# Picking 32 more early columns of the first edge stage with one-hot matmuls in the set-up

## The reference

```python
xl = (x @ W_l + b_l).reshape(n, HEADS, C)
xr = (x @ W_r + b_r).reshape(n, HEADS, C)
e = (edge_attr @ W_e).reshape(-1, HEADS, C)
g = jax.nn.leaky_relu(xl[src] + xr[dst] + e, NEG_SLOPE)
logits = jnp.einsum('ehc,hc->eh', g, att)
ex = jnp.exp(logits - segment_max(logits, dst)[dst])
alpha = ex / (segment_sum(ex, dst)[dst] + 1e-16)
out = segment_sum(xl[src] * alpha[..., None], dst)
```

## Time and profile before

| | |
|---|---|
| median of 3 runs | 5896.49 us (5888.83 to 5905.95) |
| profiled execution | 5837.42 us, span 5835.3 us |
| set-up | 0 to 135.8 us |
| edge stage 0 | from 135.8 us, last chunk near 1394 us |
| GpSimd in stage 0 | 752 gathers, 731.9 us busy, 482.6 us idle |
| TensorE over the whole program | 67% busy, VectorE 69%, ScalarE 36%, GpSimd 62% |

### The profile page before, as it was taken

One profiled execution on the slowest core, in us unless ns is written; L12 is line 12 of the kernel. 1 busy time (PEld: TensorE's weight loads), 2 busy tenths in 40 slices (PEclk: granted clock), 3 DMA queues, 4 the chain that ended last, 5 costly groups with the idle time before them and its releaser, 6 DMA issues. The chain is left out here.

```text
span 5835.3 us, 55453 instructions
## 1 busy us (share of the span) xinstructions
PE 3918.1 (67%) x16273; PEld 2718.5 (47%) x16273; DVE 4024.6 (69%) x5761; ACT 2088.4 (36%) x3734; POOL 3621.4 (62%) x3384
## 2 busy tenths in 40 slices
PE   2555555564599999999999557767733536655561
PEld 1333333333488888888888423333312422222221
DVE  3566666675599999999998557778763346555553
ACT  0455555553144444444444124444431211111111
POOL 6655555663577777777776366666655255655554
PEclk6788888886799999999999568888865767777775
DMA  7566666663588888888886333333332631211111
GB/s 276 199 220 214 217 215 223 224 224 119 203 318 311 312 316 311 315 316 309 319 309 260 83 107 108 111 110 114 101 91 88 254 101 52 57 52 53 53 51 47
DMA packets 359630, 1074.10 MB, mean 184 GB/s; under 512 B 100998, under 2 KB 124354, under 8 KB 315012
## 3 DMA queue, kind: packets, MB, share of 16 engines
q1 hardware_dynamic: 241524, 852.49, 39.0%
q0 software_dynamic: 102208, 156.10, 10.4%
q10 hardware_dynamic: 15696, 63.31, 3.2%
HBM read 678.05 MB, written 392.57 MB: 183 GB/s over the span
## 5 line engine op out<-in xcount | busy, mean ns | idle before, releaser
L1874 PE MATMUL COLS<-CF,XF 128*128 128x256 f32 x6272 | 1485.4, 380 | 6.3 <-DVE XF L1982 6.3
L1874 PEld LDWEIGHTS COLS<-CF,XF 128*128 128x128 f32 x6272 | 1134.7, 190 | 130.3 <-DVE XF L1982 6.7
L1137 ACT ACTIVATE OUT<-SC 128x576 f32<-128x576 f32 (+3 forms) x392 | 576.5, 1471 | 1333.4 <-DVE SC L1072 678.9
L1020 POOL DMA_INDIRECT G<-xl_tab,SRC x752 | 731.9, 973 | 482.6 <-DVE TURNS L1054 272.2
L1841 POOL DMA_INDIRECT G<-x_tab,SRC x784 | 780.9, 996 | 234.6 <-issue 216.0
L1020 POOL DMA_INDIRECT G<-rel_tab,REL x672 | 639.1, 951 | 424.6 <-DVE SC L1072 227.2
L1020 POOL DMA_INDIRECT G<-kv_tab,SRC x608 | 599.7, 986 | 372.8 <-issue 187.6
L1451 PE MATMUL PICK<-HOT,X 125*128 125x512 bf16 x2200 | 571.0, 418 | 276.0 <-issue 147.7
L1623 PE MATMUL MADE<-XM,W 128*128 128x512 f32 x896 | 529.5, 747 | 328.4 <-DVE XM L1711 261.8
L1261 PE MATMUL WK<-B2R,ONER 128*128 128x512 f32 x392 | 258.6, 660 | 524.1 <-ACT WKV L1314 483.5
L1451 PEld LDWEIGHTS PICK<-HOT,X 125*128 125x128 bf16 x2200 | 228.0, 105 | 603.6 <-issue 396.6
(11 more groups left out here) (310 smaller groups left out, 7086.0 us busy)
## 6 DMA issues: line engine op xcount, KB each, us to landing
SHB<-ea9t SPq DMA_DIRECT2D x196, 1024.0 KB
wkv_tab<-WKV SPq DMA_DIRECT2D x98, 1024.0 KB
WKV<-wkv_tab SPq DMA_DIRECT2D x98, 1024.0 KB
scan<-OUT SPq DMA_DIRECT2D x196, 288.0 KB
scan<-OUT ACTq DMA_DIRECT2D x98, 576.0 KB
rel_tab<-YS SPq DMA_DIRECT2D x50, 1024.0 KB
RAW<-spread SPq DMA_DIRECT2D x196, 256.0 KB
spread_q<-ZQ SPq DMA_DIRECT2D x98, 512.0 KB
```

The costliest lines, as they stand in the source:

```text
L1020: pool.indirect_dma_start(out=self.G[0][d][:, c, :], out_offset=None, in_=tab, in_offset=bass.IndirectOffsetOnAxis(ap=index[:, at:at + 1], ...
L1137: nc.scalar.activation(self.OUT[d][:, :, 0:WD], SC[b][:, 0:WD, 1:1 + C].rearrange("p r j -> p j r"), ACT.Copy).then_inc(self.copied_out, 1)
L1874: nc.tensor.matmul(acc, XF[b][:, k, edges_], CF[:, k, :], start=(k == 0), stop=False)
```

## The change

EARLY_T becomes every chunk from 1 to 95 that is no multiple of three: 64 chunks in place of 32. The stage then has 720 gathers and 64 place_early copies. XEARLY doubles. Its first 32 columns are gathered in the set-up as before. The other 32 (t = 49 to 95) are picked in the set-up, in four batches of 8 columns (1024 edges):

- SP broadcasts the 1024 source indices of a batch to all partitions (SRC8, 512 KB), ScalarE narrows them to 16 bits (ID16), and VectorE compares them with each of the 25 groups of nodes into HOT, five groups at a time, two buffers.
- x is split in three bfloat16 pieces, which lie in X3 as [high, middle] and [low, blank]. TensorE multiplies each of the two pairs by the one-hot columns, two halves of 512 columns: 20 matmuls in a pick, 5 picks in a batch, 400 matmuls in all. They are summed in PICK, which takes the two PSUM banks that FB and PR had.
- ScalarE copies PICK to TURNED (take), TensorE multiplies it by the weights stacked twice (project_picked), and VectorE adds b_l (make_picked).

The orders of the engines change with it. TensorE does picks 0 and 1 between the second and the third group of table rows, pick 2 before the last group, and all others behind the rows, with the turning and projecting of the gathered columns among them.

```diff
-EARLY_T = [2 + 3 * i for i in range(EARLY)]
+EARLY_PICKED = 4
+EARLY_T = [t for t in range(1, NCH - 2) if t % 3]
...
+                    def load_sources(i):
+                        if i:
+                            sp.wait_ge(narrowed, i)
+                        sp.dma_start(SRC8[:, :], src_first[i:i + 1, :].to_broadcast([P, 8 * P])).then_inc(src8_in, 16)
...
                         sp.wait_ge(seg_in[part], 16 * (k1 - k0))
+                        if part == 1:
+                            load_sources(1)
                         blank_spread(sp, range(3 + 2 * part, 5 + 2 * part))
                     blank_spread(sp, range(3 + 2 * len(PARTS), BLANKS))
+                    for i in range(2, EARLY_PICKED):
+                        load_sources(i)
                     sp.wait_ge(rows_made, 7)
...
+                    def compare(at):
+                        i, q = divmod(at, 5)
+                        v.wait_ge(narrowed, i + 1)
+                        if at == 0:
+                            v.wait_ge(node_known, 1)
+                        if at >= 2:
+                            v.wait_ge(read, at - 1)
+                        for k in range(5 * q, 5 * q + 5):
+                            ins = nc.vector.tensor_scalar(HOT[at % 2][N, k % 5, :], ID16[i % 2][N, :], NODE_F[N, k:k + 1],
+                                                          None, ALU.is_equal)
+                        ins.then_inc(compared, 1)
...
+                        if part == 0:
+                            v.wait_ge(x_high, 1)
+                            nc.vector.tensor_tensor(REST[:, :, :], X[:, :, :], X3[:, :, 0, 0:64], ALU.subtract)\
+                              .then_inc(x_rest, 1)
+                            compare(0)
+                        if part == 1:
+                            v.wait_ge(x_middle, 1)
+                            nc.vector.tensor_tensor(X3[:, :, 1, 0:64], REST[:, :, :], X3[:, :, 0, 64:128], ALU.subtract)\
+                              .then_inc(x_low, 1)
+                            compare(1)
...
+                        if u == 4:
+                            compare(2)
...
+                    for at in range(3, 5 * EARLY_PICKED):
+                        compare(at)
+                        if at % 5 == 1:
+                            make_picked(at // 5 - 1)
+                        if 12 <= at <= 15:
+                            make_early(at - 12)
+                    make_picked(EARLY_PICKED - 1)
...
+                    narrow(0)
+                    act.wait_ge(x_rest, 1)
+                    nc.scalar.activation(X3[:, :, 0, 64:128], REST[:, :, :], ACT.Copy).then_inc(x_middle, 1)
+                    narrow(1)
+                    act.wait_ge(x_low, 1)
+                    take(0)
+                    narrow(2)
+                    take(1)
+                    narrow(3)
...
+                    def pick(at):
+                        i, q = divmod(at, 5)
+                        pe.wait_ge(compared, at + 1)
+                        if q == 0 and i >= 1:
+                            pe.wait_ge(taken, i)
+                        for k in range(5 * q, 5 * q + 5):
+                            for piece in range(2):
+                                for half in range(2):
+                                    edges_ = slice(512 * half, 512 * half + 512)
+                                    last = nc.tensor.matmul(PICK[:, edges_], X3[N, k, piece, :], HOT[at % 2][N, k % 5, edges_],
+                                                            start=(k == 0 and piece == 0), stop=(k == K - 1 and piece == 1))
+                        last.then_inc(read, 1)
...
+                    project_rows(0)
+                    project_rows(1)
+                    pe.wait_ge(t_copied, 2)
+                    pe.wait_ge(blank, 1)
+                    pe.wait_ge(x_low, 1)
+                    pick(0)
+                    pick(1)
+                    for u in range(2, len(GROUPS)):
+                        if u == len(GROUPS) - 1:
+                            pick(2)
+                        project_rows(u)
+                    for at in range(3, 5 * EARLY_PICKED):
+                        pick(at)
+                        if at % 5 == 0:
+                            project_picked(at // 5 - 1)
+                        if 12 <= at <= 15:
+                            project_early(at - 12)
+                        if 11 <= at <= 14:
+                            turn_early(at - 11)
+                    project_picked(EARLY_PICKED - 1)
```

More of the change, by code:

```diff
@@ L58 @@
 EARLY = 32
-EARLY_T = [2 + 3 * i for i in range(EARLY)]
+EARLY_PICKED = 4
+EARLY_T = [t for t in range(1, NCH - 2) if t % 3]
 EARLY_FIRST = 4
 ROWS0_AT = [sum(C - (q in EARLY_T) for q in range(t % 4, t + 1, 4)) for t in range(NCH)]
-assert EARLY_T[-1] < NCH - 2 and EARLY % 8 == 0
+assert EARLY_T[-1] < NCH - 2 and EARLY % 8 == 0 and len(EARLY_T) == EARLY + 8 * EARLY_PICKED
 BATCHES3 = 14
@@ L243, in graph_kernel @@
         early_rows = ExitStack()
-        XEARLY = sb("XEARLY", [P, EARLY, 64], F32, early_rows)
+        XEARLY = sb("XEARLY", [P, len(EARLY_T), 64], F32, early_rows)
         BLANKS = J // 56
@@ L440, in _, with make_early @@
                     st.then(nc.vector.tensor_scalar(CARRY_AT[:, :], ST[:, 4, 2:3], float(NPAD), None, ALU.add))
[L442 to L450, removed]
-                    for i in range(EARLY // 8):
+                    def make_early(i):
                         v.wait_ge(early_done, i + 1)
@@ L465, in _, with narrow, take, copy_early @@
                           .then_inc(x_copied, 1)
-                    for i in range(EARLY // 8):
+                    nc.scalar.activation(X3[:, :, 0, 0:64], X[:, :, :], ACT.Copy).then_inc(x_high, 1)
+                    def narrow(i):
+                        act.wait_ge(src8_in, 16 * (i + 1))
+                        if i >= 2:
+                            act.wait_ge(compared, 5 * (i - 1))
+                        nc.scalar.activation(ID16[i % 2][:, :], SRC8[:, :], ACT.Copy).then_inc(narrowed, 1)
+                    def take(i):
+                        act.wait_ge(read, 5 * i + 5)
+                        if i >= 1:
+                            act.wait_ge(pick_done, i)
+                        nc.scalar.activation(TURNED, PICK[:, :], ACT.Copy).then_inc(taken, 1)
+                    def copy_early(i):
                         act.wait_ge(early_turned, i + 1)
@@ L495, in _, with project_picked, turn_early @@
                         last.then_inc(rows_done, 1)
-                    pe.wait_ge(w_early_in, 16)
-                    pe.wait_ge(x_early_in, 16 * EARLY)
-                    for i in range(EARLY // 8):
-                        if i >= 1:
+                    def pick(at):
[10 more added lines that the diff above has]
+                        last.then_inc(read, 1)
+                    def project_picked(i):
+                        pe.wait_ge(taken, i + 1)
+                        if i == 0:
+                            pe.wait_ge(weights_stacked, 1)
+                        else:
+                            pe.wait_ge(pick_made, i)
+                        for c in range(8):
+                            last = nc.tensor.matmul(PT[0][:, 64 * c:64 * c + 64], TURNED[:, c * P:(c + 1) * P], WL2[:, :],
+                                                    start=True, stop=True)
+                        last.then_inc(pick_done, 1)
+                    def turn_early(i):
+                        if i == 0:
+                            pe.wait_ge(w_early_in, 16)
+                            pe.wait_ge(x_early_in, 16 * EARLY)
+                        else:
                             pe.wait_ge(early_copied, i)
@@ L2592 @@
         "basis": a["L3_gnn_basis"],
-        "src_early": np.stack([src_cols[:, t * C + C - 1] for t in EARLY_T], axis=1),
+        "src_early": np.stack([src_cols[:, t * C + C - 1] for t in EARLY_T[:EARLY]], axis=1),
+        "src_first": np.stack([src_cols[:, t * C + C - 1] for t in EARLY_T[EARLY:]]).reshape(EARLY_PICKED, 8 * P),
         "w_early": w_early,
```

49 lines of the change are left out of this document (45 added, 4 removed).

## The result

The changed kernel has a median of 5972.62 us (5961.46 to 5979.04, 4 runs) against 5895.81 for the kernel before on the same chip: the ratio is 1.0127, 95% interval 1.0106 to 1.0148, or 77 us more. The forecast of slower was right, and 5972 lies in the range, but the step was put at 26 us, a third of what came. The profiled execution has a span of 5959.6 us.

The account below looks back on a forecast made before the run. GpSimd ends the set-up; no engine bounds stage 0 throughout, but GpSimd's gathers count one for one in its cycle. Set-up +66 and stage 0 -40 give +26 on the 5896.49 median: 5922 us, range 5865 to 5980.

Parts of the forecast that it names:

- What goes: Edge stage 0: 32 gathers fewer on GpSimd, 40 us saved, with bounds of 0 and 110.
- If the two pauses stay, each cycle shortens by 1.25 us: Stage 0's three-chunk cycle: with GpSimd's pauses of 7.33 and 1.58 us unchanged, 32 x 1.25 = 40 us go.
- Rival B: Stage 0: gathers aren't in the cycle, so fewer only lengthen GpSimd's pause; net +43 to +66 us, chance 0.15.
- What comes: Set-up: picking adds 43 us at full pace, plus 17 and 6 for TensorE's second pace, +66 in all.
- Table rows at 82: Set-up: the last table rows, ending at 77.15 before, end at about 82 with pick(2) ahead of them.
- Late signals beside the first run of gathers: Set-up, GpSimd's run until 91.2: TensorE's slow pace loses between nothing and 12 us; 6 taken.
- unknown price: Set-up: matmuls beside GpSimd's back-to-back runs might go 2.1 to 3.5 us apart, as in stage 2; 17 + 6 us.
- The objection that the table rows of before ran without gaps: Set-up: rows 2 to 6 ran beside gathers without slow-pace gaps, which spoke against that pace there; no size of its own.
- Late signals beside the scatters: Set-up, scatters ending at 134: 18 us in which 7 or 8 matmuls pass where 85 would; 17 us lost.
- D: Set-up: matmuls mostly run at the lower clock because of waits between groups; net about +75 to +90 us, chance 0.10.
- A (full pace in the set-up): Set-up: TensorE keeps its full pace, set-up +43, net +3 us, so 5900 and no difference; chance 0.20.
- C (rarer stalls): Stage 0: stalls come once per four chunks, 110 us less there, net -44, so 5852; chance 0.15.

Follow-up runs that it names:

- setup_rest: The changed kernel with a GpSimd memset of 128x1100 behind every fifth XEARLY gather and every fifth set-up scatter; 1.0074 of the kernel before, set-up 197.3 us.
- stage_all_seven: The kernel before with 7 gathers in each of chunks 1 to 95 of stage 0, placed rows being copies; 0.9859 of the kernel before, stage 0 1211.3 us.
- reorder: The changed kernel with compares from 13 ahead of make_early, pick and compare 2 behind the table rows, table stores before the last index load; 1.0092 of the kernel before.
- no_scatter: The changed kernel without the 25 set-up scatters, output not the reference's; one run of 5880.56 us, set-up 207.1 us.

## Why the forecast was a third of the result

**What goes (forecast -40, measured -10 to -25).** The failed step is "If the two pauses stay, each cycle shortens by 1.25 us". The first pause stayed. The second is the wait for L1054 of the second chunk after a stall, which hangs on ScalarE and TensorE catching up, and that got longer. The trace has the cause beside it. Before, the granted clock rises to 2.4 GHz 4.55 us after WKV restarts; after, 6.74 us, so TensorE works 2.2 us longer at 1.2 GHz, which at half the speed is 1.1 us lost, close to the gather's 1.25 (an estimate):

```profile
716.44:720.99 4.55, 3.48 (x8) 2.84 (x9) 1.09 (x3) 3.17 (x7) 0.00 (x0) 0.50 0.01 2
```

```profile
275.90:280.42 4.52, 3.44 (x8) 2.80 (x9) 1.40 (x4) 3.16 (x7) 0.11 (x1) 0.50 0.00 0
...
312.23:317.96 5.73, 4.65 (x12) 3.27 (x12) 2.60 (x4) 3.17 (x7) 1.02 (x2) 0.50 0.15 55
...
724.24:730.98 6.74, 5.67 (x14) 3.69 (x14) 2.75 (x4) 4.10 (x8) 1.89 (x2) 0.50 0.20 67
```

The first row is of the kernel before, the other three of the one after, each from a restart of WKV to the rise (columns of the earlier trace rows). The first cycle of stage 0 after is 36.33 us with a middle pause of 1.6, the forecast to 0.1 us; the next are 36.84, 37.25, 37.35, 37.51, while the pause grows to 2.6 and 2.8. A cycle that is shorter than the time from one rise of the clock to the next meets each rise a little later, until the work at 1.2 GHz has made it as long again. The rises of the trace after are 37.54 us apart from the first cycle on (280.42, 317.96), where the restarts are still 36.33 apart, and in the trace before they are too (720.99, 758.54). So the cycle came to the rises of the clock.

setup_rest has the same stage, and in its trace the rise comes early now and then (why isn't shown). Behind a rise 7.26 us after the restart the middle pause is 2.84 us and the cycle 37.48; behind one after 3.91 us the pause is 1.57 and the cycle 35.86, near the 36.3 that the forecast had for all of them:

```profile
434.21:441.47 7.26, 6.18 (x14) 3.69 (x14) 2.75 (x4) 4.20 (x8) 2.25 (x3) 0.50 0.03 6
471.69:475.60 3.91, 2.84 (x7) 2.29 (x8) 0.83 (x1) 3.16 (x7) 0.00 (x0) 0.50 0.00 0
```

```profile
450.40 0.95 POOL L1181 DMA_INDIRECT G<-xl_tab,SRC  x1 [2.84 <-DVE TURNS L1215]
...
486.24 0.95 POOL L1181 DMA_INDIRECT G<-xl_tab,SRC  x1 [1.57 <-DVE TURNS L1215]
```

So within one trace the pause follows the rise ahead of it. A kernel that holds the clock, which would settle that the one causes the other, wasn't run. Rival B named the outcome, "22 gathers would only lengthen GpSimd's pause", but not this reason, and its premise, that the gathers aren't in the cycle, is refuted by stage_all_seven.

**What comes (forecast +66, measured +87).** By the terms of the sum:
- The base held. Table rows at 82 is near what setup_rest shows (82.97 + 0.29), and a pick takes 4.48 us where 4.31 were put.
- Late signals beside the first run of gathers: I took 6 us of at most 12; it was 16 (rows made at 98.3 for 82). That I called it an "unknown price" and put half of the bound was a second step that failed, a term of the sum put too small. The objection that the table rows of before ran without gaps didn't hold once picks 0 to 2 stood ahead of the rows and between them. It isn't pick 2 alone: in reorder it stands behind the rows, and VectorE still starts the last of them at 89.33, 11.7 us after TensorE's end. Since before has the same run of gathers and no such wait, the run isn't enough by itself; what the picks add isn't shown.
- Late signals beside the scatters: 17 forecast, 10.20 measured (134.08), 14.7 with all that follows (no_scatter).
- What the sum lacked altogether: VectorE's order. compare(13) stands behind make_early(0), which waits for project_early(0), which TensorE does behind pick(12). So VectorE can't compare while TensorE picks, and each of four picks waits: 2.33 + 2.33 + 2.33 + 2.76 = 9.75 us. Just behind the second and the third of them the granted clock falls, 0.9 and 1.3 us into the pick, and each of these two picks takes 1.7 us more. reorder shows it.
- Low-clock starts after the long waits, some 1.6 us each at 134 and 198 (14.76 us for three picks, 19.06 for four), and the first compare of 2 us, make up the rest: 16 - 6 + 10 - 17 + 9.75 + 3.4 + 5.2 = 21 over the 66, for 21 measured. The terms were put together after the result, so the fit shows that nothing large is missing, and no more.

Behind the first wait of 2.33 us a pick takes 4.49 us, behind the second and the third 6.18, with the granted clock at 0.50 for a part of each. I had said under D that short waits would leave the clock up. That was wrong from the second on. The Trainium skill has the clock fall behind idle stretches ("TensorE: Matmul & The Clock Gate", section "What's actually happening"), and the trace agrees in so far as the falls come just behind waits.

**What was hidden, as forecast.** The scatters end at 134.9, ahead of TensorE (220.8) by 86 us. REST and the first compares lay in VectorE's waits: START_AT is made at 65.67, 2.2 us later than before, of which nothing reaches the end. GpSimd's gathers beside compares grew little: L388 1303 ns for 1249, L378 1015 for 1005, L398 1057 for 988, together 26 x 0.054 + 32 x 0.010 + 25 x 0.069 = 3.4 us. Only some 30 of the 100 compares lie beside them, in groups of five, and a group makes one gather or scatter about 0.25 us longer, 0.05 us for each compare:

```profile
38.19 2.06 POOL L388 DMA_INDIRECT GS<-dst_shifted,AT_SEG  x1 [0.30 <-issue]
40.56 1.19 POOL L388 DMA_INDIRECT GS<-dst_shifted,AT_SEG  x1 [0.30 <-issue]
...
44.96 0.95 POOL L388 DMA_INDIRECT GS<-dst_shifted,AT_SEG  x1 [0.30 <-issue]
```

The gather at 40.56 lies beside compare(0) (39.26 to 41.33) and takes 1.19 us for 0.95. What did hold a gather is the subtraction for REST, which reads two tiles (37.51 to 39.34): the gather that began inside it took 2.06 us and ended 0.9 us behind it. By the rule that the prediction took from the Trainium skill ("SBUF — State Buffer", section "SBUF: two separate sides") a compare of the mode in question would hold GpSimd for its full 0.48 us. These compares don't; whether they are of that mode no row shows. load_sources(3) did delay the table stores, from 77 to 114.57 and not to the 91 of the prediction, and nothing waited for them before stage 0.

**The rivals.** A (full pace in the set-up) fell, C (rarer stalls) didn't come with 22 gathers; with 18 the stalls nearly went (33.2 us of late signals for 337.1). D's condition didn't come: nearly all picks ran at 2.4 GHz.

**The base.** The prediction put its difference on the median, 59 us above the profiled execution. Some 24 to 44 us of those 59 are the stages behind edge stage 0, which are that much longer on the slower chip. The rest lies in stage 0 by the estimate above, so the cycle of 37.55 us was read on another chip than the one timed.

## What to carry to other kernels

When an engine waits for a signal and the sender's work was done long before, look at what GpSimd is doing: here the stall wasn't a matter of how many DMAs it issues but of how many without a break, and 1.5 us of rest per 8 gathers bought more than 32 gathers taken away at the price of 400 matmuls. A gain that is counted "one for one inside a cycle" needs a reason why each of the cycle's other waits stays; here the wait behind a restart at 1.2 GHz was the one that didn't. When work is handed back and forth between two engines with double buffers, write down the consumer's in-order list next to the producer's, since one wait placed a step too early undoes the second buffer.

## What the runs showed of the hardware that I had not expected

- TensorE's signals reached VectorE and ScalarE long after its own instructions had ended in the trace, always while or just after GpSimd issued indirect DMAs back to back: 11.5 us in a cycle of stage 0 before, 16.4 for the last table rows after, and 31.2 in the first stall of stage 0 before:

```profile
158.54 1.02 PE L1264 MATMUL WK<-W,HT 128*128 128x256 f32 x4
...
190.79 1.02 ACT L1314 ACTIVATE WKV<-WK 128x1024 f32<-128x1024 f32 x1 [25.91 <-remote]
```

- In stage 0 before and after, the long waits of WKV ended 1.9 to 5.1 us after GpSimd's last gather of a run. In the set-up after two signals came while it went on issuing (88.68 and 131.35), and so did some that the edge term PROJ waits for in stage 0 after (at 255.67, behind 8.1 us of waiting), so silence ends the wait but isn't the only thing that does. A break of 0.12 us did nothing, 0.70 us helped a little behind 8 gathers, 1.45 us removed most of GpSimd's own stalls, 2.12 us nearly all late signals (11.8 us of waits left of 337.1). Which part of the chip holds them back stays open. The ends of matmuls are modelled in a profile, so late work of TensorE and late signals can't be told apart. No run here takes the recording of instructions away, so whether that has a part isn't tried.
- In the traces before and after the rises of the granted clock in stage 0 came 37.54 us apart, with 23 gathers and with 22, and the cycle settled on them.
- The gain from fewer gathers isn't linear: with 23, 22, 21 and 18 in three chunks stage 0 took 1261, 1260, 1211 and 944 us (the first on a quick chip, the others on the slower one, where the first is estimated at 1274 to 1294).
- The same kernel took 5894 us on one chip and 5822 to 5828 on three others, so a difference of 1% can't be read across chips.
